# Gated cross attention and experts: the sum of squares of the third weights moves between the halves of the value product, and VectorE takes scales and maxima ahead of the moments

## The reference

```python
x = x + jnp.tanh(g_xattn[0]) * _L0_xattn_ref(ctx_1024, _layernorm(x, axis=-1), wq, wk, wv)
x = x + jnp.tanh(g_ffn[0]) * _L0_ffn_ref(_layernorm(x, axis=-1), Wg, W1, W2, W3)

# _L0_xattn_ref(q, c, wq, wk, wv)
Q = jnp.einsum('bld,dh->blh', c, wq)
K = jnp.einsum('bld,dh->blh', q, wk)
V = jnp.einsum('bld,dh->blh', q, wv)
attn = jax.nn.softmax(jnp.einsum('bch,bqh->bcq', Q, K), axis=2)
out = jnp.einsum('bcq,bqh->bch', attn, V)

# _L0_ffn_ref: TOP_K = 2, E = 8, H = 704
scores = xt @ Wg.T
topk_scores, topk_idx = jax.lax.top_k(scores, TOP_K)
gate = jax.nn.silu(jnp.einsum('td,ehd->teh', xt, W1))
up = jnp.einsum('td,ehd->teh', xt, W2)
y = jnp.einsum('teh,edh->ted', gate * up, W3)
out = jnp.einsum('te,ted->td', w, y)      # w: the scores of the chosen two, else 0
```

## Time and profile before

| what | value |
|---|---|
| median of 3 runs | 587.07 us (585.71 to 587.38) |
| profiled execution, its time | 586.03 us |
| profiled execution, its span | 584.3 us, 14520 instructions |
| busy share of the span | PE 96%, PEld 83%, DVE 54%, ACT 53%, POOL 50% |
| granted TensorE clock | 0.991 |
| attention stage | about the first 160 us of the span |

### The profile page before, as it was taken

The page is one execution under the profiler, slowest core; times in us unless marked ns, Lnnn a source line. Parts: engine busy times, 40 slices in busy tenths (PEclk is TensorE's granted clock), DMA queues, the critical chain, the costliest instruction groups (busy, mean ns, idle before and its releaser), DMA issues.

```text
span 584.3 us, 14520 instructions
## 1 busy us (share of the span) xinstructions
PE 560.0 (96%) x4641; PEld 487.6 (83%) x4641; DVE 314.8 (54%) x876; ACT 312.4 (53%) x438; POOL 290.0 (50%) x262
## 2 busy tenths in 40 slices
PE   7899998999799999999999999999999999999995
PEld 6687787888678898889889888998988898897883
DVE  3489887988888866833433433343343334333332
ACT  1787887788845554444453544445354444534441
POOL 3039898989878666633333243233324323333323
PEclk8999999999989999999999999999999999999998
DMA  7656888686524444543233322323332242322322
GB/s 232 203 169 184 282 247 267 212 285 192 173 74 137 82 101 105 147 74 66 38 48 51 54 41 46 67 39 48 50 54 41 47 66 40 47 42 44 55 31 27
DMA packets 52371, 61.49 MB, mean 105 GB/s; under 512 B 7632, under 2 KB 46160, under 8 KB 52304
## 3 DMA queue, kind: packets, MB, share of 16 engines
q1 hardware_dynamic: 34368, 38.15, 22.4%
q0 software_dynamic: 13296, 18.23, 18.8%
q10 hardware_dynamic: 4640, 4.20, 2.1%
HBM read 36.90 MB, written 23.66 MB: 104 GB/s over the span
## 4 chain that ended last, share of the span: by engine, by line
PE 69%; POOL 16%; issue 4%; DVE 4%; SPq 2%; DMA 2%; ACT 2%; POOLq 0%; DVEq 0%; ACTq 0%
PE psum L949 38%; PE psum L981 23%; POOL rows_by_expert L573 6%; PE psum L958 4%; POOL arena L583 4%; PE psum L865 3%; POOL rstd L553 2%; POOL xn2r L592 2%; DMA xa<-in_x 1%; POOL var_eps L550 1%; POOL xn2r L589 1%; POOL var_eps L551 1%; PE psum L967 1%; SPq L438 0%; DMA rows_by_expert<-xn2r,slot_i 0%
## 5 line engine op out<-in xcount | busy, mean ns | idle before, releaser
L615 POOL DMA_INDIRECT out<-w_in,id_s x71 | 129.6, 1825 | 235.4 <-ACT w_in L768 116.7
L949 PE MATMUL psum<-arena,w_hi 128*128 128x256 f16 x1408 | 212.4, 274 | 2.6 <-ACT arena L699 1.4
L949 PEld LDWEIGHTS psum<-arena,w_hi 128*128 x1408 | 137.8, 98 | 19.9 <-issue 3.4
L949 PE MATMUL psum<-arena,w_lo 128*128 128x256 f16 x704 | 135.1, 274 | 0.0
L699 ACT ACTIVATE arena<-psum 128x1024 f16<-128x1024 f16 (+1 forms) x39 | 36.9, 947 | 101.3 <-PE psum L865 101.2
L1386 DVE SCALAR_TENSOR_TENSOR arena<-psum,h_unit,arena 128x1280 f32<-128x1280 f32 x32 | 49.6, 1550 | 63.5 <-PE psum L949 63.5
L573 POOL DMA_INDIRECT rows_by_expert<-xn2r,slot_i x64 | 71.5, 1118 | 17.9 <-issue 17.3
L949 PEld LDWEIGHTS psum<-arena,w_lo 128*128 x704 | 69.2, 98 | 8.3
L821 PE MATMUL psum<-arena 128*128 128x264 f32 x256 | 64.5, 397 | 2.5 <-DVE halves L1057 2.2
L744 ACT ACTIVATE arena<-psum,w_unscale 64x256 f32<-64x256 f32 x32 | 14.9, 467 | 87.6 <-PE psum L949 87.6
L981 PE MATMUL psum<-w_hi,arena 128*128 x396 | 59.1, 273 | 1.0 <-ACT arena L758 1.0
(11 more groups left out here) (194 smaller groups left out, 854.2 us busy)
## 6 DMA issues: line engine op xcount, KB each, us to landing
xa<-rows_by_expert SPq DMA_DIRECT2D x71, 136.0 KB, 2.3
w_in<-in_W1T SPq DMA_DIRECT2D x8, 704.0 KB, 5.0
w_in<-in_W2T SPq DMA_DIRECT2D x8, 640.0 KB, 5.0
w_in<-in_W3T SPq DMA_DIRECT2D x8, 640.0 KB, 6.1
arena<-in_ctxT SPq DMA_DIRECT2D x16, 256.0 KB, 6.3
xa<-in_x SPq DMA_DIRECT2D x16, 256.0 KB, 6.8
out<-xa ACTq DMA_DIRECT2D x16, 256.0 KB, 4.3
out<-w_in,id_s POOLq DMA_INDIRECT x71, 4.2
```

The source lines that it names most:

```text
L615: pool.indirect_dma_start(out=out[:, :], out_offset=bass.IndirectOffsetOnAxis(ap=id_s[:, t8:t8 + 1], axis=0), in_=y_s[:, t8 % 4, :], in_of ...
L949: ins = pe.matmul(flat_ps[:, j * N2:(j + 1) * N2], w12[w_part][:, c, bass.ds(e * (2 * H) + j * P, P)], xg_t[:, k, x_part, c, :], start=(q ...
```

## The change

Two edits of order; no instruction is added or removed.

1. TensorE: `weight_sum3` is no longer called after the scores in odd steps but inside `values(m)` for even m (the same step, since `values(n - 1)` is called in step n), between the two halves of the product. It still waits for ScalarE's squares (`s_sq3`) and for `s_v_copied`.
2. VectorE: in each step `first_moments(n + 2)` and `second_moments(AT_STEP[n + 1])` stand behind `scales`, `maxima` and `slots` instead of in front of `scales`. The `second_moments` further down in the step, for a block that has just been finished, stays where it was.

```diff
@@ values(m), TensorE
                 product(o_ps, probs_t, v_s[:, m % 2], tiles=(0,))
-
+                if m % 2 == 0:
+                    weight_sum3(m // 2)
                 pe.wait_ge(s_half, min(m + 2, B))
@@ the step loop, TensorE
                 product(sc_and_xw_ps, x_t, z_s).then_inc(s_sc, 1)
-                if k == 1:
-                    weight_sum3(n // 2)
                 if n - 1 in AT_STEP:
@@ the step loop, VectorE
-                if live(n + 2):
-                    first_moments(n + 2)
-                if n + 1 in AT_STEP and AT_STEP[n + 1] < n - 1:
-                    second_moments(AT_STEP[n + 1])
                 if live(n):
 
                     dve.wait_ge(s_ssq, n + 1)
@@
                     maxima(n)
                 if n - 1 in AT_STEP:
                     slots(AT_STEP[n - 1])
+                if live(n + 2):
+                    first_moments(n + 2)
+                if n + 1 in AT_STEP and AT_STEP[n + 1] < n - 1:
+                    second_moments(AT_STEP[n + 1])
                 if live(n) and k == 1:
```

## The result

The changed kernel took 583.62 us (median of 20 runs, 581.98 to 589.18) against 587.18 us (20 runs, 585.52 to 590.13) for the kernel before. The ratio is 0.9947, 95% interval 0.9928 to 0.9966: 3.1 us less, by more than the 0.3% that the prediction calls the limit. It lies in the stated range, 0.1 us above its lower end of 583.5, and outside the likeliest case's own 585.3 to 588.8; "no change" was the forecast.

The account below looks back on a forecast made before the run. GpSimd was taken to set the pace of steps 2 to 13. Terms of -1.0, three zeros and +0.9 summed to -0.1 us against the profiled execution, giving 587.0 us from a 587.07 median; range 583.5 to 590.2.

Parts of the forecast that it names:

- likeliest case: The forecast of 587.0 us itself, own range 585.3 to 588.8, chance 0.46, counted as no change.
- What bounds the kernel: Steps 2 to 13: GpSimd sets the pace, about 27.5 us per three steps; without it little over 4 us winnable.
- one missed collision plus a little: Lower end, 583.5 us, of the 8-in-10 range: one of GpSimd's long L583 no longer meets VectorE's low halves.
- The start: Step 0: exponents 1.7 us earlier, GpSimd starting at 41.2 instead of 42.26; -1.0 us, bounds 0.5 and 1.7.
- TensorE's edit: Third weights' sum later: most of 4.2 us of TensorE waits removed, but costed at nothing in the GpSimd-bound stretch.
- Steady steps and collisions: Steps 5, 8, 11: choice 0.85 us later, made up, 0; low halves hitting GpSimd differently, 0, bounds -5.0 to +5.0.
- so no new wait: VectorE's scales for third weights come some 0.9 us later, but moments, 0.94 us, stand before them: no added wait.
- The end: Step 14: second moments of block 9 fall behind VectorE's rstd wait, with no slack after it; +0.9 us.
- Rival 2: VectorE becomes the bound: moments behind rstd wait cost 0.95 us in steps 5, 8, 11, 14; 589.9 us; chance 0.20.
- Rival 1: VectorE's low halves miss both long L583 of GpSimd: 582.0 us, with one missed 584.5; chance 0.24.
- Rival 3: Waits go, nothing else; start's lead lost to a late load in first 40 us; 587.1 to 588; chance 0.10.
- The marks named: Profile signs of being right: exponents about 20.9, GpSimd wait ending 41.2, experts at 160.7, rstd waits in four steps.

Follow-up runs that it names:

- step0_new: The kernel before with VectorE's new order in step 0 alone, TensorE and steps 1 to 15 as before; ratio 0.9913 (0.9881 to 0.9945), 5.2 us less.
- step0_old: The changed kernel with VectorE's old order in step 0, moments of block 2 first; ratio 1.0041 (1.0022 to 1.0059) to the kernel before.
- pe_only: The kernel before with only TensorE's edit, VectorE as before; ratio 0.9987 (0.9954 to 1.002).
- before_again: The kernel before, unchanged, run and profiled once more; ratio 0.999 (0.996 to 1.002).
- pe_step0: The kernel before with TensorE's edit and VectorE's new order in step 0 alone; ratio 0.9903 (0.986 to 0.9945).
- dve_only: The kernel before with only VectorE's edit, in all steps, TensorE as before; ratio 0.9992 (0.9952 to 1.0033).

## Why the prediction was right or wrong

**What bounds the kernel: held for the kernel before, not throughout for the changed one.** The experts' stage did not move (423.3 against 423.6 us), and GpSimd has no wait for another engine of more than 0.30 us from 37.29 to the last scatter of block 7. But the chain of waits no longer runs along it all the way. In the kernel before it ends the attention stage with the last scatter (chain: start, us):

```profile
151.75 2.48 DMA rows_by_expert<-xn2r,slot_i
```

In the changed kernel it leaves GpSimd for good at the rstd of step 11 and from there stays for the most part with VectorE, nbias first, then moments, choice and low halves, up to the experts:

```profile
114.27 1.05 POOL rstd L553
...
115.42 0.06 DVE nbias L1160
...
121.97 1.73 DVE w_lo L1083
...
156.38 2.02 DVE w_lo L1076 x2
```

That removing the waits of ScalarE and TensorE there brings little by itself held too: the four of the earlier trace rows fell by 12.9 us and the stretch got no shorter. That the measured time still lies in the range is luck: the lower end was "one missed collision plus a little", and no collision was missed. The start gave some 4 us more than forecast (5.2 by step0_new against 1.0), and the later steps cost what had been put at nothing.

**The start, forecast at -1.0 us: this is the step that failed, by its size.** The mechanism is as written: ScalarE's wait for w_scale is gone in step 0, and the exponents wait for the maxima. I had them 2.94 us behind the scores' start (20.85 - 17.91); it is 2.99. What failed is the sentence "exponents ... 1.7 us earlier", and with it the upper bound "1.7 (all of the exponents' lead)". Both subtract a fixed 17.91 from a fixed 22.59, read from one execution in which the value weights landed late and the first products ran at 1.2 GHz. Only 22.59 was fixed, by x's landing at 19.92. The scores' start moves between 14.2 and 19.1 us from execution to execution of kernels with the same loads, and the wait of 4.89 us for x in the earlier trace rows hid that. With the new order the early executions keep their lead. The profiled pair differs by 5.4 us in the exponents and 5.0 us at GpSimd's first L583; in the medians I estimate it at 4.4 to 5.5 us, the 3.1 of the result and what the rest costs (1.3 by the means of the table's last column, 2.4 by step0_old's ratio); step0_new, which has nothing but this, measured 5.2. The profile of before, read for what else the landing held up, would have given the bound: without TensorE's wait of 2.27 us and with full clock in its first two groups (0.46 and 1.22 us less) the scores start up to 3.9 us earlier, and 1.7 + 3.9 makes a lead of 5.6.

How much of the lead is lost up to GpSimd I had at 0.7 us (of 1.7, 1.0 kept). From the exponents to L583 it is 22.38 us in the kernel before and 22.77 in the changed one: 0.4 lost.

**TensorE's edit, forecast at 0: by the marks wrong by 1 to 2 us.** Beside old later steps it brings 1.9 us (138.9 to 136.9; 1.2 against the first profile alone), in three executions; the ratio of pe_only alone does not tell it from nothing. "The work that hides it is GpSimd's" was too simple, since GpSimd's work isn't of fixed length. From L583 to the scatter it takes 105.9 us in the three kernels with this edit and old later steps, 106.8 to 107.2 in the four with neither. The scatters of 2.29 us are the difference. In pe_only (timeline of GpSimd) they read:

```profile
85.27 1.38 POOL L573 DMA_INDIRECT rows_by_expert<-xn2r,slot_i  x1 [0.30 <-issue]
...
86.95 1.43 POOL L573 DMA_INDIRECT rows_by_expert<-xn2r,slot_i  x1 [0.31 <-issue]
```

Two of 1.4 us in place of one of 2.29 and one of 0.96 are 0.4 us less, and this happens twice. TensorE's earlier sum lets VectorE go a little earlier against GpSimd: the second low half starts 0.45 us behind a scatter here (85.72 and 85.27) and 1.00 us behind it in the kernel before (87.37 and 86.37). With that the price of the meeting changes. The part up to L583 is 0.5 us less (21.84, against 22.4 in three of those four and 23.3 in before_again).

**Steady steps and collisions, forecast at 0 each: near, for a sum of larger parts.** In the changed kernel L583 to the scatter takes 107.55 us against 106.78. GpSimd's groups in that stretch, before (44.97 to 151.75; busy us, mean ns, idle before):

```profile
L573 POOL DMA_INDIRECT rows_by_expert<-xn2r,slot_i x32 | 37.5, 1171 | 8.8 <-issue 8.5 <-ACT arena L672 0.3
L583 POOL TENSOR_SCALAR arena<-xa,mv,rstd 128x256 f32<-128x256 f32 x16 | 24.5, 1534 | 0.1
L553 POOL TENSOR_TENSOR rstd<-var_eps,neg_half 128x4 f32<-128x4 f32 (+1 forms) x11 | 11.3, 1029 | 0.9
...
L550 POOL TENSOR_SCALAR var_eps<-mv 128x2 f32<-128x2 f32 x7 | 4.4, 632 | 0.5
```

and after (40.00 to 147.55):

```profile
L573 POOL DMA_INDIRECT rows_by_expert<-xn2r,slot_i x31 | 32.1, 1036 | 8.5 <-issue 8.2 <-DVE mv L1183 0.3
L583 POOL TENSOR_SCALAR arena<-xa,mv,rstd 128x256 f32<-128x256 f32 x16 | 26.0, 1631 | 0.1
L553 POOL TENSOR_TENSOR rstd<-var_eps,neg_half 128x4 f32<-128x4 f32 (+1 forms) x11 | 13.1, 1189 | 0.9
...
L550 POOL TENSOR_SCALAR var_eps<-mv 128x2 f32<-128x2 f32 x7 | 5.8, 834 | 0.5
```

The scatters are 4.4 us cheaper (one of the 32 starts on the window's edge; 0.96 us is added back for it), L583 1.5, L553 1.8 and L550 1.4 us dearer: +0.3 us, and with the short L551 (+0.4) +0.7, which is the 0.8 us by which the stretch grew. The collisions did not fall away, they moved from scatters to arithmetic. Both L583 of 4.9 us stayed, where I had one of them moving on to var_eps and rstd, and two more took 3.2 us (at 74.40 and 130.04) instead of 2.4.

The sentence "so no new wait", on the scales of the third weights, is wrong. ScalarE waits for them in front of L678 in four places, 3.9 us in all. It takes the new order of the later steps: step0_old has the same 3.9 us, pe_only and pe_step0 have none.

The page "SBUF — State Buffer" of the Trainium skill, section "Who interferes with whom", would have VectorE's low halves cost scatters nothing. By that inference moving the low halves could not make scatters cheaper; their mean fell from 1171 to 1036 ns.

**The end, forecast at +0.9 us: held, a little less.** With step 14 alone in the old order the way from the scatter to the experts is 9.2 us instead of 9.8, +0.6; the whole way from the exponents differs by 0.5. Against the first profile of the kernel before the end grew by 0.9 us (8.95 to 9.82).

**Rival 2, VectorE as the bound: true in its mechanism, at a third to two thirds of its price.** It gave 3.8 us for the moments behind the wait for rstd in steps 5, 8, 11 and 14. Putting those four back gains 1.3 us on average by the marks (140.1 to 138.8) and 2.6 us by the medians on one chip. VectorE waits for rstd there in two of the four, as here in step 5:

```profile
59.78 0.16 DVE L1160 TENSOR_TENSOR nbias<-nmax,rstd 128x2 f32<-128x2 f32 x1 [1.78 <-POOL rstd L553]
```

In the chain of waits of the whole kernel, before and then changed, its share has grown from 4% to 13%, as the rival has it:

```profile
PE 69%; POOL 16%; issue 4%; DVE 4%; SPq 2%; DMA 2%; ACT 2%; POOLq 0%; DVEq 0%; ACTq 0%
...
PE 71%; DVE 13%; POOL 7%; issue 4%; ACT 3%; DMA 1%; SPq 0%; POOLq 0%; ACTq 0%; DVEq 0%
```

The other steps, which I had at nothing, cost more than these four: 138.8 - 136.9 = 1.9 us. Which of them was not tried. The chain says where the cost lies: in pe_step0 it is back on GpSimd up to the last scatters (POOL 16%, DVE 1%), so it is VectorE, with the moments behind the bias, that has become late. By which wait it does so stays open. Beside TensorE's edit, then, the new order in steps 1 to 15 costs 3.2 us (140.1 - 136.95), and TensorE's edit gives back 1.9 of it; without that edit it costs 2.2 (141.0 in dve_only).

**Rival 1** gave the right sign and nearly the right time (582 to 584.5) for a reason that isn't so: no L583 of 4.9 us was missed. **Rival 3** is refuted by the start. The sign that I had named for rival 2, GpSimd waiting for mv, did not show it: there is one such wait, of 0.3 us, though VectorE is on the chain.

**The marks named:** right were the first (no wait of ScalarE in step 0), the third weights' wait at about 1 us, GpSimd without waits, and two long L583. Wrong were exponents at 20.9 (17.22), GpSimd's wait ending at 41.2 (37.29), experts at 160.7 within 1 us (157.37), no wait for halves (0.8 us is left in two of them), and rstd waited for in four steps (two).

## What to carry to other kernels

When the first instruction in an engine's queue waits for a load, look at what stands behind it that doesn't need the load: here 4.9 us of an idle VectorE held back all of step 0, and moving one call in one step gained at least as much as the whole change (5.2 us against 3.1, with overlapping intervals). Don't subtract two times of one profile when one of them is set by a load and the other follows a start that varies: take such a mark as a distance from what releases it, and ask what the wait has been hiding. An order that pays in the one step where the engine is held by a load may cost in the others (3.2 us here by the marks), so try it step by step.

## What the runs showed of the hardware

**The first 18 us vary by themselves.** The value weights' load is issued at 3.36 us in the changed kernel's profile, and in the executions of kernels with the same loads TensorE first used it at 8.4 to 12.0 us. In six of these twelve executions TensorE's clock fell to 1.2 GHz at the end of the wait or less than 1 us behind it (in dve_only it was 1.00 up to 10.60 and 0.50 from 10.80), and the first product of eight passes took 3.1 to 3.5 us instead of 1.89; a wait of 2.25 us was followed by full clock in before_again, one of 1.55 us by half clock in dve_only, so the wait's length alone does not tell which. The latter's clock (0.50) reads:

```profile
10.80:12.80 2.00, 2.00 (x6) 1.59 (x5) 0.68 (x1) 0.00 (x0) 0.00 (x0) 0.50 0.90 298
```

**Chips differ in the experts' stage.** It took 422 to 425 us on the chips where the kernel before needs 587 us, and 437 to 445 us on the other two, with the same code of this stage and a clock of 0.98 to 0.99 (0.99 to 1.00 on the faster chips). For before_again:

```profile
162.08:598.80 436.72, 415.68 (x3870) 364.33 (x3870) 191.08 (x425) 189.06 (x234) 175.01 (x120) 0.99 0.32 59
```

TensorE is busy for 415.7 of 436.7 us there and for 413.2 of 423.6 in the earlier trace rows; what it waits for more was not looked into.

**GpSimd holds VectorE as well.** An instruction of VectorE (L1144) that takes 0.19 us in the median of its 16 takes 1.17 us beside GpSimd's L592, which runs from 78.34 to 79.51, and the same again at 134.03 (timeline of VectorE in the changed kernel):

```profile
69.66 0.19 DVE L1144 TENSOR_TENSOR placed<-hot,place 128x32 f32<-128x32 f32 x1
...
78.38 1.17 DVE L1144 TENSOR_TENSOR placed<-hot,place 128x32 f32<-128x32 f32 x1
```
